# Adaptive norm, attention and feed-forward on one core: sums, fc1 units and splits put elsewhere, high parts made by ScalarE

## The reference

```python
x = x + attn(cond(x))          # one layer of attention on a conditioned norm
x = x + ffn(cond2(x))          # a feed-forward on a mixed two-layer network
# cond:  h = relu(x W1[l] + b1[l]); y = x + h W2[l] + b2[l]; layernorm(y) * gamma[l] + beta[l]   (l by sequence)
# attn:  16 query heads of 16, one key head and one value head, causal, softmax in float32, then Wf, bf
# cond2: h = gelu(x fc1 + b) (256 -> 1024); 192 outputs by fc2, 64 by the expert of the sequence
# ffn:   silu(x w1 s1) * (x w2 s2) (256 -> 1024); gelu(. h1 sh1); gelu(. h2 sh2) (1024 -> 1024); . w3 s3 (-> 256)
#        w1, w2, h1, h2, w3 hold -1, 0 and 1
```

## Time and profile before

| | |
|---|---|
| median of three runs | 1170.0 us (1169.46 to 1173.75) |
| the profiled execution | 1171.29 us, of which the trace's span is 1169.6 us |
| PE busy | 1119.1 us, 96% |
| DVE busy | 822.5 us, 70% |
| ACT busy | 595.1 us, 51% |
| POOL busy | 216.7 us, 19% |
| granted PE clock, mean | 0.993 |

### The profile page before, as it was taken

The page is one execution under the profiler, slowest core; times in us unless marked ns, Lnnn a source line. Parts: engine busy times, 40 slices in busy tenths (PEclk is TensorE's granted clock), DMA queues, the critical chain, the costliest instruction groups (busy, mean ns, idle before and its releaser), DMA issues.

```text
span 1169.6 us, 18787 instructions
## 1 busy us (share of the span) xinstructions
PE 1119.1 (96%) x6148; PEld 890.4 (76%) x6178; DVE 822.5 (70%) x1440; ACT 595.1 (51%) x989; POOL 216.7 (19%) x266
## 2 busy tenths in 40 slices
PE   4899999999996899999999999999999999999998
PEld 3577777777774688888888888888888888888886
DVE  3876776776764766886568875688756877568775
ACT  1355556556555443344256654566545665455653
POOL 2243343343344534533100000000000000000000
PEclk9999999999998999999999999999999999999999
DMA  4342111121153264554504443044430444304420
GB/s 120 111 150 66 51 60 56 51 61 55 51 174 118 93 219 169 199 191 172 200 34 162 145 162 124 19 162 143 162 122 22 161 144 161 116 28 141 145 90 37
DMA packets 66764, 135.97 MB, mean 116 GB/s; under 512 B 13792, under 2 KB 28016, under 8 KB 66544
## 3 DMA queue, kind: packets, MB, share of 16 engines
q1 hardware_dynamic: 57696, 114.49, 29.8%
q10 hardware_dynamic: 9024, 20.97, 5.0%
HBM read 107.65 MB, written 30.41 MB: 118 GB/s over the span
## 4 chain that ended last, share of the span: by engine, by line
PE 81%; DVE 9%; issue 5%; ACT 1%; SPq 1%; POOL 1%; DMA 1%; DVEq 0%; ACTq 0%; POOLq 0%
PE bank L1512 35%; PE bank L1474 10%; PE bank L1524 5%; PE bank L1450 4%; PE bank L1233 4%; PE bank L1214 3%; DVE g_parts L1010 3%; PE bank L1299 2%; DVE neg_max L872 2%; PE bank L1291 2%; PE bank L1196 2%; PE bank L1254 2%; PE bank L1180 2%; PE bank L1444 1%; PE bank L1217 1%
## 5 line engine op out<-in xcount | busy, mean ns | idle before, releaser
L1512 PE MATMUL bank<-op_lo,w_ring 128*128 128x512 f32 x896 | 348.6, 389 | 0.0
L1512 PE MATMUL bank<-op_hi,w_ring 128*128 128x512 f32 x896 | 348.6, 389 | 0.0
L1046 DVE TENSOR_TENSOR op_lo<-x_blk,op_hi 128x512 fp32r<-128x512 f32 x288 | 193.7, 684 | 30.4 <-ACT op_hi L745 30.3
L745 ACT ACTIVATE op_hi<-x_blk 128x512 fp32r<-128x512 f32 x288 | 162.8, 620 | 73.5 <-PE bank L1512 69.3
L1512 PEld LDWEIGHTS bank<-op_lo,w_ring 128*128 128x128 f32 x896 | 168.2, 188 | 35.0
L1512 PEld LDWEIGHTS bank<-op_hi,w_ring 128*128 128x128 f32 x896 | 168.2, 188 | 34.9
L872 DVE TENSOR_REDUCE neg_max<-bank 128x2 f32<-128x512 f32 (+1 forms) x192 | 126.0, 685 | 51.0 <-remote 41.9
L598 ACT ACTIVATE p<-bank 128x512 f32<-128x512 f32 x192 | 111.3, 599 | 69.5 <-PE bank L1233 65.6
L1233 PE MATMUL bank<-q_t,keys 128*128 128x512 f32 x192 | 94.4, 509 | 11.8 <-ACT p L598 6.7
L769 ACT ACTIVATE x_blk<-x_blk,scales 128x512 f32<-128x512 f32 x96 | 69.3, 722 | 67.0 <-DVE x_blk L1099 28.9
L1474 PE MATMUL bank<-tile_hi,ffn_w 128*128 128x512 f32 x256 | 101.5, 396 | 0.0
(11 more groups left out here) (124 smaller groups left out, 1868.9 us busy)
## 6 DMA issues: line engine op xcount, KB each, us to landing
w_ring<-hid_scratch SPq DMA_DIRECT2D x112, 512.0 KB, 4.7
hid_scratch<-comb ACTq DMA_DIRECT2D x8, 1792.0 KB, 6.3
comb<-in_hid_d ACTq DMA_DIRECT2D x6, 768.0 KB, 5.5
xt<-in_x_t SPq DMA_DIRECT2D x16, 256.0 KB
xtok<-in_x_tok SPq DMA_DIRECT2D x16, 256.0 KB
resid<-in_x_t SPq DMA_DIRECT2D x16, 256.0 KB, 3.1
x_scratch<-x SPq DMA_DIRECT2D x16, 256.0 KB, 2.6
tile_in<-x_scratch SPq DMA_DIRECT2D x8, 512.0 KB, 4.1
```

What stands on the lines that cost most here:

```text
L745: nc.scalar.activation(op_hi[:, o % OP_RING, k], x_blk[:, operand_home(o), k], ACT.Copy).then_inc(s["op_hi"], 1)
L1046: nc.vector.tensor_tensor(op_lo[:, o % OP_RING, k], x_blk[:, operand_home(o), k], op_hi[:, o % OP_RING, k].bitcast(F32), ALU.subtract).the ...
L1512: last = mm(banks[first_bank + m][:, :], w, read(v[:, q % OP_RING, k, :]), start=k == 0 and v is op_hi and i not in (P2, P3), stop=k == KB ...
```

## The change

Five edits, all in the two first phases.

1. POOL's four sums of a chunk become separate calls `combine(c, i)`. Those of chunks 0 and 1 are spread over iterations B - 3 and B - 2, between the `causal` calls; in tile t POOL now sums chunk t + 2, not t + 1. ACT's `finish_chunk` calls stand where they stood.
2. PE computes fc1 units 0 and 1 at the start of iteration B - 1, ahead of its scores, and unit 5 ahead of `attention_transposed`, unit 6 ahead of `project_out`.
3. DVE's `split_x(0)` moves from the end of iteration B - 2 to after its second maximum, and `split_fc2b` and `split_fc2a` from the end of iteration B - 1 to its beginning, with one more wait (`values_moved`).
4. ACT makes the high part `g_hi` in all tiles, right behind each gelu (for which it waits by a semaphore); DVE makes only the low part.
5. In tile 0, ACT's `attention_out` and DVE's `attention` stand one unit later.

```diff
@@ -512,6 +512,7 @@
...
             def iteration(b, odd, front, maxima, softmax, tail):
+                last_front, last_maxima = front and isinstance(b, int) and b == B - 3, maxima and not front
                 if maxima:
@@ -519,30 +520,46 @@
...
                 if softmax:
-                    for f in range(1, 4):
-                        causal(b, f)
+                    causal(b, 1)
+                if last_front:
+                    combine(0, 0)
+                elif last_maxima:
+                    combine(0, 3)
+                if softmax:
+                    causal(b, 2)
+                if last_front:
+                    combine(0, 1)
+                elif last_maxima:
+                    combine(1, 0)
+                if softmax:
+                    causal(b, 3)
                 if front:
...
                     move_keys(b + 2, odd, softmax)
+                if last_front:
+                    combine(0, 2)
+                elif last_maxima:
+                    combine(1, 1)
                 if softmax:
...
                     high_again(b + 2, 1)
-                if maxima and not front:
-                    combine(0)
-
-            def combine(c):
-
-                pool.wait_ge(comb_loaded[c % 2], 32 * (c // 2 + 1))
+                if last_maxima:
+                    combine(1, 2)
+                    combine(1, 3)
+
+            def combine(c, i):
+
+                if i:
+                    pool.wait_ge(s["comb_made"], 4 * c + i)
+                else:
+                    pool.wait_ge(comb_loaded[c % 2], 32 * (c // 2 + 1))
+                out, in0, in1, op = [(S1, A21, A22, ALU.add), (S2, S1, A11, ALU.subtract), (S3, A11, A21, ALU.subtract), (S4, A12, S2, ALU.subtract)][i]
                 w = comb[c % 2]
-                made = [(S1, A21, A22, ALU.add), (S2, S1, A11, ALU.subtract), (S3, A11, A21, ALU.subtract), (S4, A12, S2, ALU.subtract)]
-                for i, (out, in0, in1, op) in enumerate(made):
-                    if i:
-                        pool.wait_ge(s["comb_made"], 4 * c + i)
-                    nc.gpsimd.tensor_tensor(w[:, out, :], w[:, in0, :], w[:, in1, :], op).then_inc(s["comb_made"], 1)
+                nc.gpsimd.tensor_tensor(w[:, out, :], w[:, in0, :], w[:, in1, :], op).then_inc(s["comb_made"], 1)
 
@@ -553,7 +570,7 @@
...
 
-            def cond2_tile(t, more):
+            def cond2_tile(t):
                 pool.wait_ge(s["expert_loaded"], 16 * BT * (t + 1))
@@ -563,11 +580,12 @@
...
                     nc.gpsimd.tensor_tensor(fc2b_lo[:, :, j, SHARED - P:P], exp_raw[:, j], fc2b_hi[:, :, j, SHARED - P:P].bitcast(F32), ALU.subtract).then_inc(s["expert_split"], 1)
-                if more:
-                    combine(t + 1)
+                if t + 2 < CHUNKS:
+                    for i in range(4):
+                        combine(t + 2, i)
 
             for t in range(TILES):
-                cond2_tile(t, t < TILES - 1)
+                cond2_tile(t)
             pool.wait_ge(s["expert_split"], HEAD + BT * TILES)
@@ -685,7 +703,7 @@
...
                         products_out(B - 1, True)
-                    elif t == 0 and m == 4:
+                    elif t == 0 and m == 5:
                         attention_out(B - 1)
@@ -696,6 +714,8 @@
...
                     nc.scalar.activation(g_raw[:, m % 2, :], bank[:, :], ACT.Gelu, bias=fc1_bias[:, m:m + 1]).then_inc(s["raw_ready"], 1)
+                    act.wait_ge(s["raw_ready"], KH * t + m + 1)
+                    nc.scalar.activation(g_hi(m), g_raw[:, m % 2, :], ACT.Copy).then_inc(s["hi_ready"], 1)
 
@@ -912,6 +932,11 @@
...
                     add_adapted(b + 2)
+                elif maxima:
+                    split_x(0)
+                else:
+                    split_fc2b()
+                    split_fc2a()
                 if maxima:
@@ -940,11 +965,6 @@
...
                     queries_of(b + 2, 1)
-                if maxima and not front:
-                    split_x(0)
-                if not maxima:
-                    split_fc2b()
-                    split_fc2a()
 
@@ -952,6 +972,7 @@
...
                 dve.wait_ge(s["qv_mm"], NT * B)
+                dve.wait_ge(s["values_moved"], B)
                 for j in range(BT):
@@ -1006,14 +1027,12 @@
...
                 for m in range(KH):
-                    dve.wait_ge(s["raw_ready"], KH * t + m + 1)
-                    nc.vector.tensor_copy(g_hi(m), g_raw[:, m % 2, :]).then_inc(s["hi_ready"], 1)
                     dve.wait_ge(s["hi_ready"], KH * t + m + 1)
                     nc.vector.tensor_tensor(g_lo(m), g_raw[:, m % 2, :], g_hi(m).bitcast(F32), ALU.subtract).then_inc(s["act_ready"], 1)
-                    if is_first(t) and m == 1:
+                    if is_first(t) and m == 2:
                         attention(B - 1, 0)
                         attention(B - 1, 1)
-                    if is_first(t) and m == 4:
+                    if is_first(t) and m == 5:
                         add_residual(B - 1)
@@ -1330,6 +1349,9 @@
...
                     products(b - 1, other, True, maxima)
+                if softmax and not maxima:
+                    first_tile(0)
+                    first_tile(1)
                 if softmax:
@@ -1344,8 +1366,6 @@
...
                     queries_transposed(b + 1, 1, 1, tail)
-                if softmax and not maxima:
-                    first_tile(0)
                 if softmax:
@@ -1370,8 +1390,6 @@
...
                     attention_transposed(b - 1)
-                if softmax and not maxima:
-                    first_tile(1)
                 if maxima:
@@ -1415,10 +1433,10 @@
...
             first_tile(4)
+            first_tile(5)
             attention_transposed(B - 1)
-            first_tile(5)
+            first_tile(6)
             project_out(B - 1, False)
-            first_tile(6)
             first_tile(7)
```

## The result

The changed kernel takes 1157.71 us (median of 4 runs, 1157.43 to 1159.08) beside 1170.55 (median of 4, 1169.46 to 1173.75) for the kernel before, a ratio of 0.9888 [0.9867, 0.9909]. The forecast was 1155.5 us in a range of 1150 to 1161, faster with a chance of 0.95. Its profiled execution took 1157.89 us, with a span of 1156.2 at a mean granted clock of 0.996.

A forecast was written before the change was run, and what follows sets the result against it. PE bounds the kernel, with slack only ahead of the feed-forward, in late attention and the tiles. Gains 5.7 + 5.9 + 4.2 - 0.6 = 15.2 us give 1156.1 or 1154.8, said as 1155.5 us, range 1150.0 to 1161.0.

The forecast's parts named there:

- The units ahead: Start of iteration B - 1: two fc1 units, 2.74 us, run without waiting and cover PE's 2.40 us wait for maxima.
- ACT freed: Iteration B - 1: chunk 0 already summed, ACT stores near 363, is ready for exponentials about 367.5, no longer holds up scores.
- The price of the early store: Ahead of the scores in B - 1: the earlier store delays SP's maxima; first scores at 371.8, a wait of 3.3 us.
- the rival of shared queues: Store and SP's moves take turns: maxima land before 368.5, gain 19.0 us, 1151.7 us; chance 20%.
- The rest of the iteration: B - 1 from first scores: 8.0 us for twelve exponentials plus 0.5 for the clock, ending at 380.3; gain 5.7 us.
- the store costs more: Rival: maxima at 373.9 and low clock through the scores, another 1.0 us; gain 12.1 us, 1158.6 us; chance 13%.
- From there to tile 1: End of B - 1 to tile 1: 5.17 us wait and 1.5 half clock go, 0.8 comes; net gain 5.9 us.
- The tiles: Tiles 1 to 6: 0.70 us of waiting a tile goes, 22.92 to 22.22 us; gain 4.2 us.
- Sums within attention: Iterations B - 3 and B - 2: six POOL sums slow `normalise`, which PE awaits; 0.6 us lost, bounds 0 and 2.5.
- ACT the bound: Rival, in the tiles: gelu and copy pair takes 2.07 us, tiles 2.4 us longer than 22.92, 1177 us; chance 3%.
- signs of being wrong: First scores before 369 or after 374, a tile over 22.6 us, or gelus later than one PE unit apart.
- The total: Whole kernel: 15.2 us off the profiled 1171.29 gives 1156.1, off the median 1170.0 gives 1154.8; said 1155.5 us.

The follow-up runs named there:

- the late store: Changed kernel, but ACT issues the store of chunk 0 inside iteration B - 1, behind the exponentials of u = 1; 1153.35 us, ratio 0.9838.
- the second profile: Profile of the changed kernel run again without an edit; median 1156.41 us, ratio 0.9862.
- the three kernels with the late store: Changed kernel with chunk 0's store issued later: alone 1153.35 us; with two sums moved off `norm` 1151.39; with the second products copy also one gelu earlier 1150.26.
- the extra copy: Changed kernel with one more ACT copy of each gelu, into a tile nobody reads, ahead of the high part; 1166.45 us, ratio 0.9952.
- the kernel of the last run: Changed kernel with chunk 0's store issued late, two sums moved off `norm`, and tile 0's second products copy one gelu earlier; 1150.26 us, ratio 0.9815.

## Why the prediction was right, step by step

**The units ahead.** Right: two units, 2.74 us, and no wait ahead of them. With the units put back, the wait grows by 2.94.

**ACT freed.** Right in both halves. The store is issued at 364.17 with no wait for `comb`, the scores are no longer held, and putting the sums back brings the wait for ACT back (7.59 us).

**The price of the early store.** The mechanism was right, and it was the disputed step. I took 371.8 for the maxima, 6.1 us behind the last products; it was 5.8 (367.56 to 373.36), and the wait 2.79 for 3.3. That the size came out so near is in part luck. The sum written for it, 2.1 MB at 0.30 MB/us from 364.2, gives 371.2 and not 371.8, and it leaves out the second 256 KB of SP, the store of x (`x_scratch`), though the rival of shared queues mentions it. In the trace q10 and q1 move 1.84 and 0.55 MB, 2.39 in all, in the 7 us from 365 to 372, and the scores start 1.4 us later: more bytes, at a higher rate (0.34 MB/us), and a hand-over at the end, which nearly cancel. Shared queues (1151.7 us) are out: q10 has 100% of the engines' time from 365 to 369, and only the late store (1153.35) comes near what that rival promised. The Trainium skill ("DMA: Bandwidth & Descriptors", Queues, rings and completion order) has the engines take turns between queues, a packet of descriptors at a time. The trace does not show such turns on this scale: q1 moved nothing for 4 us here (365 to 369), as it had moved nothing in the earlier trace rows. No run varied the size of the store's descriptors, so whether very long turns explain it stays open.

**The rest of the iteration.** This is the term that was mis-sized, at 8.0 + 0.5 us. It measured 9.83, and 10.59 in the second profile. At a steady full clock it is 8.41 (the three kernels with the late store agree to 0.01), so 0.4 us was left out of the work and the clock cost 1.4 to 2.2 us instead of 0.5. I had allowed 0.5 us for the clock behind a wait of 3.3 us. That is half of the rival "the store costs more", whose landing time (373.9) did not come but whose clock did. Had this term been right, iteration B - 1 would have gained 6.0 instead of 4.7, as the maxima came 0.3 us sooner than forecast.

**From there to tile 1.** 26.56 us for 26.7. The wait for `att` is gone, and the late copy cost 0.59 for 0.8. That the early splits and ACT's high parts bring it together hides that one is nearly enough: with the high parts back on DVE and the splits early PE waits 0.37 us for `att`, with the splits back and the high parts on ACT 1.66 us, and with the high parts alone 1.57. The forecast gave the two together, and together they hold. The new places of units 5 and 6, of `attention_out` and of `attention` were not varied, so what they bring is open.

**The tiles.** 22.17 us for 22.22. High and low parts, which answer to the earlier trace rows:

```profile
L716 ACT ACTIVATE g_raw<-bank,fc_bias x64: 667/688/692, 386.7 to 553.9; 128x512 f32<-128x512 f32 x64
L718 ACT ACTIVATE g_parts<-g_raw x64: 631/634/638, 387.5 to 554.6; 128x512 fp32r<-128x512 f32 x64
L1031 DVE TENSOR_TENSOR g_parts<-g_raw,g_parts x64: 676/693/1745, 388.1 to 555.3; 128x512 fp32r<-128x512 f32 x64
```

and POOL's sums in tile 1:

```profile
422.21 6.95 POOL L562 TENSOR_TENSOR comb<-comb 128x512 f32<-128x512 f32 x4 [8.34 <-DMA comb<-in_hid_d]
```

The sums start 422.21 - 409.75 = 12.5 us into the tile, as said. What I had not seen is that the 4.5 us are paid for twice over: each of the two edits wins them alone. I argued them as one step and never asked whether half of it would do.

**Sums within attention.** -0.55 for -0.6, and from the place named: `norm` beside a sum. PE waits 1.31 us for it, and a wait of 0.67 us for the maxima in iteration B - 2, which the kernel before has at 349.83, is covered by that delay. The sums themselves take 1.27 us there, not 1.57. The 0.6 was a choice between bounds of 0 and 2.5, so its nearness is luck.

**ACT the bound.** Rightly unlikely. In the second half of a tile low parts follow each other every 1.25 us (1.24 or 1.25 in DVE's timeline), less than the 0.69 + 0.63 of the pair, so gelu and copy overlap a little and the semaphore between them costs nothing. One of the signs of being wrong did come, gelus later than one PE unit (1.37) apart:

```profile
434.88 0.69 ACT L716 ACTIVATE g_raw<-bank,fc_bias 128x512 f32<-128x512 f32 x1
...
436.68 0.69 ACT L716 ACTIVATE g_raw<-bank,fc_bias 128x512 f32<-128x512 f32 x1 [0.45 <-DVE g_parts L1031]
...
438.39 0.69 ACT L716 ACTIVATE g_raw<-bank,fc_bias 128x512 f32<-128x512 f32 x1 [0.35 <-issue]
```

The third and fourth gelu of a tile start 1.80 and 1.71 us after the one before. The third waits for DVE's first low parts, two of which take 2.29 us, and PE does not wait for any of it. The sign was put too strictly. That a slower pair does bind was shown by the extra copy.

**The total.** 14.7 us in the part that counts for 15.2: the rest of the iteration took 1.3 more (9.83 for 8.5), and the other terms gave 0.8 back (0.3 the maxima, 0.2 the way to tile 1, 0.3 the tiles). The profiled execution lies 1.8 us over the 1156.1 worked out for it; 1.28 of that is the start of the span, before anything changed, which no term could hold.

## What to carry to other kernels

When a change moves a bulk transfer, look at which small transfers are issued within the next microseconds on another queue and who waits for them: here the same store, issued 6.8 us later in the work, was worth 4.5 us. Count a wait of a few microseconds of PE with the half clock that may follow it, here half its length again or more (1.4 to 2.2 us behind 2.8). And where two edits cure one wait, price each alone: the move to ACT gave 9.5 of the 14.7 us alone, and nothing measurable on top of the others, since the late sums and the early splits had taken the same waits away.

## What the runs showed of the hardware that was not expected

- PE waits 2.79 us and works again at 373.36; the granted clock is still 1.00 from 372 to 374, 0.77 in 374 to 376, 0.50 in 376 to 378 and 0.87 in 378 to 380. It is seen to fall only after work has resumed, and in the second profile of the same kernel it stays low some 2 us longer.
- While the store has the engines, SP's issue of `resid` takes 1.35 us instead of 0.62 and its four issues of maxima 4.17 us instead of 2.77: in these runs issuing into a queue that stood still took longer.
- DVE's `norm`, which reads SBUF, takes 2.02 us for two beside one POOL sum and 0.72 without. The Trainium skill ("SBUF — State Buffer", Who interferes with whom) states an exclusive lock, for a whole instruction, of the ports that the two engines share; the 1.30 us more are about the sum's own 1.27, which agrees.
- The start of the program, up to the fourth `m_t`, varied by 4 us over thirteen profiles in code that no edit touches, nearly as much as the tiles' whole term. Part of it is the clock: from 20 to 40 us the granted clock is 0.84 to 0.85 in both profiles of the changed kernel (107.73 and 107.84) and 1.00 in the late store's (105.00). The rest stays open: the kernel of the last run had 1.00 up to there and 107.29.
